# Scale, shift and relu of the kept edge rows in halves of a unit (896 columns) on ScalarE

## The reference

```python
x_src = h[src]
x_dst = h[dst]
e = (x_dst - x_src) @ theta_w.T + x_src @ phi_w.T
e = jax.nn.relu(_bn(e, bn0_g, bn0_b))        # batch norm over all edges, then relu
e = e @ fc1_w.T
e = jax.nn.relu(_bn(e, bn1_g, bn1_b))        # again over all edges
agg = jax.ops.segment_sum(e, dst, num_segments=n)
x = agg / jnp.maximum(cnt, 1.0)[:, None]
return jax.nn.relu(x + h)
```

## Time and profile before

| | us |
|---|---|
| median of 3 runs | 12800.6 |
| profiled execution | 12812.4, its span 12810.4 |
| the two passes in it | from about 11812 to 12775 |
| DVE, PE, ACT busy over the span | 6552.3, 3639.8, 2402.6 |
| ACT L1783, 1040 instructions | 761.2 busy |

### The profile page before, as it was taken

The page is one execution under the profiler, slowest core; times in us unless marked ns, Lnnn a source line. Parts: engine busy times, 40 slices in busy tenths (PEclk is TensorE's granted clock), DMA queues, the critical chain, the costliest instruction groups (busy, mean ns, idle before and its releaser), DMA issues. The chain is left out here.

```text
span 12810.4 us, 93838 instructions
## 1 busy us (share of the span) xinstructions
PE 3639.8 (28%) x14310; PEld 2391.1 (19%) x14311; DVE 6552.3 (51%) x12405; ACT 2402.6 (19%) x6410; POOL 7622.7 (60%) x7838
## 2 busy tenths in 40 slices
PE   2212223332122233258510000000421111112987
PEld 1102222221012222224310000000221111111433
DVE  6446666664466666630245566665522222223877
ACT  1113233331123333300000000000000000000877
POOL 4667777766767777700047677777057677775013
PEclk7555666655566556679755555555655555555999
DMA  2264434452644444537314644445025533334776
GB/s 58 62 74 94 101 96 106 108 101 60 74 88 100 101 108 108 97 139 260 114 56 111 104 112 112 112 112 104 2 80 96 104 105 104 107 104 113 260 245 222
DMA packets 833811, 1413.84 MB, mean 110 GB/s; under 512 B 184676, under 2 KB 616266, under 8 KB 820952
## 3 DMA queue, kind: packets, MB, share of 16 engines
q0 software_dynamic: 277904, 662.94, 26.2%
q1 hardware_dynamic: 114696, 415.29, 9.4%
q10 hardware_dynamic: 441152, 335.02, 8.9%
HBM read 1057.62 MB, written 355.03 MB: 110 GB/s over the span
## 5 line engine op out<-in xcount | busy, mean ns | idle before, releaser
L818 POOL DMA_INDIRECT ring<-gat_table,index x3640 | 3632.7, 998 | 1229.7 <-issue 1043.2
L818 POOL DMA_INDIRECT ring<-b_table,index x1820 | 1730.4, 951 | 669.8 <-issue 525.8
L818 POOL DMA_INDIRECT ring<-kv_table,index x1820 | 1720.7, 945 | 591.1 <-issue 517.2
L949 PE MATMUL pairs<-hot_lo,hot_hi 128*128 128x128 f32 x6272 | 951.7, 325 | 1377.0 <-ACT hot_lo L979 1375.9
L949 PEld LDWEIGHTS pairs<-hot_lo,hot_hi 128*128 128x128 f32 x6272 | 925.0, 239 | 1430.5 <-issue 1429.0
L979 ACT ACTIVATE hot_lo<-hot_lo,wt 128x128 f32<-128x128 f32 x3136 | 933.9, 387 | 1310.9 <-DMA raw<-in_edges_dram,rid 1140.2
L1628 DVE TENSOR_TENSOR tb<-bt,att 128x1792 f32 x130 | 263.2, 2025 | 1663.6 <-DVEq L106 1663.6
L943 PE MATMUL pairs<-nil 128*128 128x512 bf16 x784 | 389.1, 597 | 2130.8 <-ACT dstage L988 2086.2
L1051 DVE TENSOR_TENSOR first<-ring,p 128x396 f32<-128x396 f32 (+1 forms) x910 | 478.4, 574 | 959.9 <-DVEq L106 953.5
L1650 PE MATMUL bt<-ident,ring 128*128 128x128 f32 x1820 | 416.7, 421 | 1932.2 <-PEq L106 1932.2
L1110 ACT ACTIVATE p<-x 128x56 f32<-128x56 f32 (+1 forms) x390 | 98.2, 252 | 4398.4 <-DVE x L1043 4398.4
(11 more groups left out here) (366 smaller groups left out, 8089.9 us busy)
## 6 DMA issues: line engine op xcount, KB each, us to landing
kept_ring<-kept SPq DMA_DIRECT2D x260, 896.0 KB, 4.6
dense_weights<-dstage ACTq DMA_DIRECT2D x196, 1024.0 KB
mat<-dense_weights SPq DMA_DIRECT2D x98, 1568.0 KB, 6.2
kept<-tb ACTq DMA_DIRECT2D x132, 896.0 KB, 3.8
ring<-gat_table,index POOLq DMA_INDIRECT x3640
ring<-kv_table,index POOLq DMA_INDIRECT x1820
ring<-b_table,index POOLq DMA_INDIRECT x1820
index<-slot_src SPq DMA_DIRECT2D x536, 4.8 KB
```

The source lines that it names most:

```text
L818: pool.indirect_dma_start(self.ring[:, r * UG + i, :], None, self.table, bass.IndirectOffsetOnAxis(self.index[:, half, at:at + 1], 0)).the ...
L949: mm = pe.matmul(self.ps[:, b, i * P:(i + 1) * P], self.hot_hi[:, 4 * b + i, :], self.hot_lo[:, 4 * b + i, :], start=False, stop=False, sk ...
```

## The change

In `act_unit` ScalarE does half a unit in one instruction: it waits for two counts of `r4_free`, takes both, writes two neighbouring quarters of `r4` (896 columns) and counts `relued` up by two. TensorE and VectorE still take and free quarters, one count each, as before. `r4` keeps its size.

```diff
     def act_unit(self, act, r):
         claim(act, self.loaded[r], 16)
-        for q in range(2 * S):
-            claim(act, self.r4_free)
-            act.activation(self.r4[:, q, :], self.slots[:, r, q * QW:(q + 1) * QW], ACT.Relu,
-                           bias=self.coef[:, 1:2], scale=self.coef[:, 0:1]).then_inc(self.relued, 1)
+        for h in range(S):
+            act.wait_ge(self.r4_free, 2)
+            act.sem_inc(self.r4_free, -2)
+            act.activation(self.r4[:, 2 * h:2 * h + 2, :].rearrange("p q c -> p (q c)"),
+                           self.slots[:, r, h * W7:(h + 1) * W7], ACT.Relu, bias=self.coef[:, 1:2],
+                           scale=self.coef[:, 0:1]).then_inc(self.relued, 2)
```

## The result

| | before | after |
|---|---|---|
| median, us | 12801.07 (6 runs) | 12925.43 (6 runs) |
| ratio | | 1.0097, 95% interval 1.0084 to 1.0110 |
| first pass in the profiled execution, us | 453.6 | 524.5 |
| second pass | 486.1 | 534.0 |
| us per unit, plain part of the first pass | 3.01 | 3.54 |

The kernel is slower by 124 us; the forecast was 112, with a range that holds the result. A pass is counted here from the start of ScalarE's first activation to the start of VectorE's last instruction on a unit, each time in one profiled execution. The two passes together lost 118.8 us.

A forecast was written before the change was run, and what follows sets the result against it. TensorE bounds the first pass; in the second, handing back two PSUM banks adds to its 3.00 us. Terms 53 + 10 + 48 + 0.7 = +112 us on 12800.6 give 12,913 us, range 12,865 to 12,955.

The forecast's parts named there:

- TensorE is the bound, ScalarE only follows: First pass: TensorE needs 3.00 us per unit; ScalarE keeps its pace with 0.1 us to spare per quarter.
- The loop of a half, 3.53 us: Both passes: matmuls, freeing, ScalarE's refill and handing over of half a unit take 3.53 us against TensorE's 3.00.
- The second half is the late one, with one wait per unit: Both passes: TensorE waits some 0.5 us ahead of each unit's second half, next to none ahead of its first.
- Plain part of the first pass, +53: First pass outside start and own batches: 100 units at 3.53 instead of 3.00 us, +53 us, bounds +37 and +63.
- Second pass, +48: Second pass: 97 units lose 0.44 us, 12 in the last band 0.27, band switches +2; bounds +28 and +58.
- the bank's wait: Second pass: waiting for two PSUM banks costs 0.09 to 0.25 us per unit; lies inside the new wait, not added.
- Own batches, +10: First pass, seven rounds where VectorE is away: +1.5 us per round, +10 in all, bounds 0 and +20.
- The restart: First pass, after TensorE idles 4.74 us in an own batch: second quarter's wait and longer instruction add about +0.7 us.
- The ring still covers: Rival, both passes: a half's loop fits into 3.00 us, so not slower, 12,801 us; chance 0.08.
- Only half is paid: Rival: late halves are made up where TensorE finds the other ready; lower bound +65, 12,866 us; chance 0.08.
- The clock falls: Rival: TensorE's waits lower its clock; 13,413 us if throughout, 12,975 if a tenth of the time; chance 0.06.

The follow-up runs named there:

- two r4: Changed kernel with r4 of two units instead of one in the first pass, second pass as changed: +49.8 us over before, ratio 1.0039.
- Without the slot's 0.09: Changed kernel, but at a unit's last quarter VectorE counts r4_free before tb_free, in both passes: +102.1 us over before, ratio 1.0079.
- handing on later: Kernel before, 448-column instructions each waiting for one quarter, but both quarters of a half handed on together: +38.3 us over before, ratio 1.0029.
- the bank counted first: Kernel before, but in the second pass VectorE counts bank_free, then r4_free, then tb_free: −10.2 us against before, ratio 0.9990.

## Why the prediction was right, point by point

- *TensorE is the bound, ScalarE only follows.* Right. With two r4 ScalarE's busy time fell by 23% at the same 3.01 us per unit. What the change saves on ScalarE was estimated at 146 us; its busy time on these lines fell by 173, from 761.2 to 588.3, and was worth nothing, as said.
- *The loop of a half, 3.53 us.* Right, measured 3.54, and each of its terms can be read in the trace: 1.74, 0.37, 1.13, 0.30. The instruction is 1.133 us and not the 1.12 of the own batch's row.
- *The second half is the late one, with one wait per unit.* Right: ScalarE's waits alternate 1.00 and 0.28, TensorE's groups are of eight matmuls. Without the slot's 0.09 the unit fell to 3.45.
- *Plain part of the first pass, +53.* Measured 100 × (3.543 − 3.007) = 54.
- *Second pass, +48.* Measured 534.0 − 486.1 = 47.9. Its parts are right as well: the usual units lost 42 us (43 forecast), the last band's 3 (3). That the bank's wait would lie inside the new one was right.
- *Own batches, +10.* The term that was mis-sized. A round, from behind one own batch to behind the next, took 22.73 us against 20.41 in the mean of the first six, so seven cost 16. The restart was forecast at +0.7 and is 5.51 − 4.74 = 0.77. The rows of one round:

```profile
11842.40 7.29 PE L1829 MATMUL e<-r,fc 128*128 128x448 f32 x12 [5.51 <-DVE stats L1863]
11849.99 3.24 PE L1829 MATMUL e<-r,fc 128*128 128x448 f32 x8 [0.30 <-DVE stats L1863]
11853.53 1.74 PE L1829 MATMUL e<-r,fc 128*128 128x448 f32 x4 [0.30 <-DVE stats L1863]
```

  Two waits follow. Over six rounds the two units that hold them are together 0.96 longer than before. The prediction took them as partly paid by the late restart; they are paid nearly in full. The unit right behind the restart is 0.60 longer. Its slow matmuls hide ScalarE's work, as forecast, but more of its work falls at the slow clock: of the stretch at 1.2 GHz 4.8 us lie behind the restart in place of 3.8, which at half speed is 0.5 us. That is the step that the prediction left out. The stretches themselves add up to the same 37.5 us in the seven rounds of both profiles; with one profile of each, it stays open how much of the shift the change brings and how much is chance.
- *The ring still covers.* Refuted by the rows above. *Only half is paid*: refuted; the unit takes the whole 3.54. *The clock falls*: refuted; with TensorE issuing 588 matmuls in 260 us, 85% of its pace, and one wait of 0.54 us per unit, the granted clock was 1.00 throughout 11980 to 12240. The Trainium skill, TensorE: Matmul & The Clock Gate, section A second HAM failure mode: psum-queue depth-cycling, has short idles between groups of matmuls bring swings of the clock; in the plain part of this kernel they didn't.
- *The sum.* 54 + 16 + 48 + 1 = 119 by the profiles, 124 by the medians. The 5 us between them aren't explained, and lie well within the interval (1.0084 to 1.0110 is 108 to 141 us).

## What to carry to other kernels

Before making an instruction wider, write down the loop that its buffer sits in: reading, seeing, freeing, refilling, handing on. A wider instruction in a ring of the same size lengthens it at both ends: it waits for more to be free (alone 0.17 us per unit here, as handing on later did alone), and it runs longer before it hands anything on (another 0.37); the fixed cost that it saves counts only where that engine is the bound. An engine that looks full may only be keeping pace with the one that is: compare its busy row with the pace at which it runs when it has a queue (0.65 us here against 0.75). And where several engines are all partly idle, count what each gets done in a stretch rather than how long it is busy.

## What the runs showed that I had not expected

- A full row can hide a wait: TensorE read as busy for all of the stretch, 0.0 idle, at 657 matmuls in 260 us, 5% under its pace of 693.
- The second pass of the kernel before ran at two paces, 3.09 us and in the last band 3.26, with the same instructions; with the bank counted first they became 3.01 and 3.17. In the last band TensorE waits twice per unit in place of once. There VectorE's first instruction behind its loop's branch comes 0.31 to 0.32 us after the branch, in all 12 of its returns; in 97 of the other returns it comes after 0.21. The second wait costs 0.09, and the slower first matmul behind it 0.08, together the 0.17 between 3.09 and 3.26. No run isolates this branch, and why it takes longer in the last band stays open.
